# Twelve staging slots for the weights, checks made on the staged copy, and an earlier norm for the second batch

## The chip, the cores and the metric

The kernel runs on one core of a Trainium2 chip. A core has five engines that run their own instruction streams and meet at semaphores: PE (matmul), DVE (vector), ACT (activation), POOL (GpSimd), and SP, whose queue issues the DMAs here. The metric is the device time of one execution in microseconds (us); of several executions the median is given. The program is one launch, from the inputs in device memory to the output in device memory.

## What is computed

The input `x` has 16 batches of 512 rows by 512 columns. Each row is normalized; the result feeds a causal attention with 16 heads of 32 and, side by side with it, a gated feed-forward layer with 1408 inner columns. Both results are added to `x`:

```python
xn = _layernorm(x, axis=-1)
x = x + attn(xn, w_qkv, b_qkv, w_out, b_out) + ffn(xn, gate_w, up_w, down_w, gate_s, up_s, down_s)
# attn: qkv = xn @ w_qkv.T + b_qkv; softmax(q k / sqrt(32) + causal) v; out @ w_out.T + b_out
# ffn:  (silu((xn @ gate_w.T) * gate_s) * ((xn @ up_w.T) * up_s)) @ down_w.T * down_s
```

`gate_w`, `up_w` and `down_w` hold only -1, 0 and 1. The kernel computes with pairs of 16-bit floats (a high part and the rest); the three ternary matrices need only one 16-bit part, and the kernel checks while it runs that they fit into it. If a check fails, a slow general path is run instead (`general_path`).

## The kernel before, in words

`fast_path` writes one program for each engine. The work of the attention is cut into 640 **slots**, `n = 0 .. 639`: a batch is 40 slots, 4 groups `G` of 4 heads with 10 slots (`U`) each. In slot `n` PE makes one 512-wide set of scores (`scores`, L247), DVE takes the row maximum (`maximum`, L515), ACT the exponential (L436), DVE the reciprocals (L504, L506), ACT the high part of the probabilities (`high`, L428) two slots later and DVE the low part (`low`, L525). SP turns the probabilities with DMA transposes (`turn_p`, L826), and PE multiplies them by `v` (`av`). All other work hangs on slots by tables that are written out by hand: `f_at` (the gate and up products with `tanh`, `hidden`, `split_hidden`), `qk_at`, `v_at`, `av_at`, `o_at`, `d_at` (the down product), `norm_at` (the norm of the next batch), `res_at` (the load of the residual). Every engine goes through the slots in the same order and through the tables in a fixed order inside a slot, and waits in that order; so what one instruction waits for holds up all that stands behind it on its engine, the DMA issues of SP included.

**The weights** come as 49 chunks of 128 by 512 fp32 (256 KB each), in the order of `chunks`: eight chunks of `w_qkv`, then gate, up and down chunks by turns, with four more of `w_qkv` among them, and four of `w_out` last. Before the change they go through eight staging slots (`NST = 8`: the four quarters of `xnT[1]`, then `res[0..3]`). SP loads chunk `n` when chunk `n - 8` is finished (`load_weight`, L798 to L801). A "split" chunk gets its high part from ACT (L387) and its low part from DVE (L483) or POOL (L691, L693). A "plain" chunk (gate, up, down) is copied to 16 bits by ACT (gate and down, L387) or POOL (up, L687). Chunks 0 to 16 are worked on ahead of slot 0, the others two to a slot from slot 0 on (`w_slot`, `W_FIRST = 17`).

**The check** of a plain chunk (`check_plain`, L557 to L565) stands far later: in batches 1 to 11 there are three per batch, at slots 22, 28 and 34 of the batch (`check_at`). Each loads the chunk a second time into an `xin` buffer (issued by SP four slots earlier, L882), compares it on DVE with the 16-bit copy (L564), and takes the largest magnitude of the copy (`tensor_reduce`, L565).

**The norm** of batch `b` for tile `t` (128 rows): load of `x` into `xin` four slots ahead (L882), statistics on DVE (L487 to L491), the root on POOL (L735), two slots later the scaling (`scaled`, L497), then the high part on POOL (L789), the low part on DVE (L660), and at slot + 5 a DMA transpose into `xnT[b % 2]` (`turn_x`, L812). For `b >= 2` the four tiles stand at slots 0, 4, 8 and 12 of the batch before; for `b = 1` at slots 12, 14, 16 and 18 of batch 0. The first product that needs batch 1 is `qk` at slot 23.

**The stack**: the scores of a group of four heads read `stk[G % 2]`, which SP fills by 12 small DMAs from `qkp` (`stack`, L814 to L819), four in each of slots 2, 3 and 4 of the group before; one semaphore counts all twelve. The stack of group 0 is issued ahead of slot 0, between the loads of chunks 12 and 13.

## Time and profile before

| what | value |
| --- | --- |
| median of 3 runs | 2051.01 us (2050.69 to 2054.36) |
| the profiled execution, its own time | 2044.33 us |
| its span, first to last instruction | 2041.0 us |
| mean granted clock of PE, share of full | 0.98 |
| PE, DVE, ACT, POOL busy, share of the span | 93%, 83%, 65%, 49% |
| the chain that ended last: PE, DVE, SP's queue, DMA, ACT | 39%, 28%, 14%, 8%, 6% |
| slot 0 begins (first `maximum`) | 49.19 us |

The span is some 3 us shorter than the time of the same execution; what lies around it is the launch and the end. "Busy" counts the time in which an engine has an instruction in work, and DMA issues do not count. A window in the profile is a stretch of the span; below, a slot begins where its first `maximum` (L515 on DVE) begins, and windows "of slots" are cut there. The granted clock is given as a share of 2.4 GHz.

### The profile page before, as it was taken

How to read it: one execution, taken by the hardware profiler on the slowest of the kernel's cores; microseconds unless marked ns; L12 is line 12 of the kernel's file. 1: busy time of each engine (PE TensorE's matmuls, PEld its weight loads, DVE VectorE, ACT ScalarE, POOL GpSimd, SP SyncE). 2: the span in 40 equal slices, each digit the busy share in tenths (PEclk: the TensorE clock that was granted, in tenths of full speed). 3: DMA queues.
4: the chain of work that ended last, by engine and by line, in shares of the span. 5: the costliest groups of instructions: out<-in, count | busy, mean ns of one | idle time of the engine just before them, and what ended most of it. 6: DMA issues, size and time to landing. Idle time of an engine off the chain costs nothing.

```text
span 2041.0 us, 43778 instructions
## 1 busy us (share of the span) xinstructions
PE 1891.5 (93%) x14978; PEld 1225.1 (60%) x14978; DVE 1695.2 (83%) x5066; ACT 1330.5 (65%) x3723; POOL 1007.2 (49%) x1389
## 2 busy tenths in 40 slices
PE   5679999999999999999999999999999999989986
PEld 3447566665666656566665666656566665756663
DVE  3668888888888888888888898888888788888885
ACT  3747676665766667666666766666666666767673
POOL 5554554554554454554544545454554555454342
PEclk8889999999999999999999999999999999999998
DMA  6866867778677776868869787777877768676674
GB/s 196 222 125 128 185 133 163 153 136 177 134 165 146 149 162 136 179 133 163 153 135 181 139 163 150 145 175 129 180 136 161 142 137 175 130 171 122 132 147 94
DMA packets 832981, 310.24 MB, mean 152 GB/s; under 512 B 756464, under 2 KB 789232, under 8 KB 832752
## 3 DMA queue, kind: packets, MB, share of 16 engines
q1 hardware_dynamic: 832752, 307.39, 73.4%
q8 instruction: 119, 1.95, 0.4%
q14 instruction: 110, 0.90, 0.1%
HBM read 55.59 MB, written 16.78 MB: 35 GB/s over the span
## 4 chain that ended last, share of the span: by engine, by line
PE 39%; DVE 28%; SPq 14%; DMA 8%; ACT 6%; issue 4%; POOL 0%; DVEq 0%; ACTq 0%; POOLq 0%
PE bank L245 39%; SPq L819 10%; DVE phl L525 8%; DMA pt<-phl 7%; DVE bank L515 5%; ACT phl L428 4%; DVE fh L537 3%; DVE ft L533 2%; DVE small L506 2%; ACT bank L436 2%; DVE res L549 1%; SPq L826 1%; DVE small L487 1%; DVE xhl L660 1%; SPq L812 1%
## 5 line engine op out<-in xcount | busy, mean ns | idle before, releaser
L428 ACT ACTIVATE phl<-bank,small 128x512 f16<-128x512 f32 (+3 forms) x1024 | 500.2, 531 | 322.4 <-DVE small L506 217.7
L436 ACT ACTIVATE bank<-bank,small 128x512 f32<-128x512 f32 (+3 forms) x1024 | 514.4, 503 | 225.5 <-DVE small L515 218.6
L525 DVE SCALAR_TENSOR_TENSOR phl<-bank,small,phl 128x512 f16<-128x512 f32 (+3 forms) x1024 | 525.3, 544 | 102.1 <-ACT phl L428 98.3
L515 DVE CUSTOM_DVE_ANT_0 bank<-bank,mask 128x512 f32<-128x512 f32 (+3 forms) x1024 | 486.0, 505 | 109.3 <-PE bank L245 109.1
L718 POOL TENSOR_SCALAR ht<-fh 128x256 f16<-128x256 f32 x352 | 142.2, 404 | 602.1 <-DVE fh L537 602.1
L245 PE MATMUL bank<-xnT,wg 128*128 128x256 f16 x2816 | 368.0, 274 | 15.8 <-POOL wu L687 6.0
L245 PE MATMUL bank<-xnT,wu 128*128 128x256 f16 x2816 | 368.4, 274 | 0.0
L245 PE MATMUL bank<-xnT,wqkv 128*128 128x512 f16 x1536 | 355.9, 382 | 11.1 <-DMA xnT<-xhl 8.1
L245 PE MATMUL bank<-wd,ht 128*128 128x512 f16 x1408 | 330.4, 392 | 0.0
L245 PEld LDWEIGHTS bank<-xnT,wg 128*128 128x128 f16 x2816 | 262.2, 98 | 82.6 <-issue 13.2
L245 PEld LDWEIGHTS bank<-xnT,wu 128*128 128x128 f16 x2816 | 277.1, 98 | 33.5
L245 PE MATMUL bank<-stk 96*128 96x512 f16 (+3 forms) x1024 | 247.4, 303 | 51.8 <-DVE phl L525 50.9
L720 POOL TENSOR_TENSOR ht<-fh,ht 128x256 f16<-128x256 f32 x352 | 246.4, 700 | 29.4
L245 PEld LDWEIGHTS bank<-xnT,wqkv 128*128 128x128 f16 x1536 | 148.4, 98 | 179.9 <-issue 12.9
L245 PEld LDWEIGHTS bank<-wd,ht 128*128 128x128 f16 x1408 | 141.3, 101 | 167.9 <-issue 21.3
L436 ACT ACTIVATION_READ_ACCUMULATOR bank<-bank,small 128x1 f32 x1024 | 209.9, 205 | 0.0
L394 ACT ACTIVATE ft<-bank,small 128x256 f32<-128x256 f32 x352 | 168.5, 483 | 57.4 <-PE bank L245 56.9
L537 DVE SCALAR_TENSOR_TENSOR fh<-bank,small,ft 128x256 f32<-128x256 f32 x352 | 170.3, 484 | 39.2 <-DVE ft L533 1.4
L245 PE MATMUL bank<-wqkv,xnT 128*128 128x256 f16 x1536 | 179.8, 274 | 15.6 <-DMA xnT<-xhl 15.6
L245 PE MATMUL bank<-wout,att 128*128 128x512 f16 x768 | 176.1, 379 | 10.5 <-DVE res L549 7.6
L245 PEld LDWEIGHTS bank<-wqkv,xnT 128*128 128x128 f16 x1536 | 150.2, 98 | 40.2 <-DVE wqkv L483 15.5
L245 PEld LDWEIGHTS bank<-stk 96*128 96x128 f16 x1024 | 96.5, 99 | 126.2 <-DVE phl L525 68.9
(95 smaller groups left out, 1911.8 us busy)
## 6 DMA issues: line engine op xcount, KB each, us to landing
stk<-qkp SPq DMA_DIRECT2D x768, 64.0 KB, 2.1
res<-in_x_dram SPq DMA_DIRECT2D x64, 256.0 KB, 3.1
out_dram<-res SPq DMA_DIRECT2D x64, 256.0 KB, 2.4
xin<-in_x_dram SPq DMA_DIRECT2D x60, 256.0 KB, 3.2
pt<-phl SPq DMA_TRANSPOSE x512, 3.7
xin<-in_gate_dram SPq DMA_DIRECT2D x11, 256.0 KB, 3.3
xin<-in_up_dram SPq DMA_DIRECT2D x11, 256.0 KB, 3.3
xin<-in_down_dram SPq DMA_DIRECT2D x11, 256.0 KB, 3.4
```

The source lines that it names most:

```text
L245: mm = lambda o, lhs, rhs, start, stop, **k: eng.matmul(o, lhs, rhs, start=start, stop=stop, skip_group_check=True, **k)
L394: eng.activation(ft[f % 3][:, :], bank[4 + f % 2][:, 0:256], ACT.Tanh, scale=gsh[:, k:k + 1]).then_inc(a_ft, 1)
L428: i = eng.activation(phl[qt][:, j % 2, 0], pb[:, off:off + W], ACT.Copy, scale=st_r[:, c:c + 1])
L436: i = eng.activation(pb[:, off:off + W], pb[:, off:off + W], ACT.Exp, bias=st_m[:, c:c + 1], scale=-1.0, accum_out=st_s[:, c:c + 1])
L506: eng.tensor_scalar(st_r[:, c0:c0 + 4], st_r[:, c0:c0 + 4], PS, None, op0=ALU.mult).then_inc(v_rec, 1)
L515: i = eng.tensor_tensor_reduce(out=bk[:, off:off + W], in0=bk[:, off:off + W], in1=mask[:, 512 - W:512], scale=-(32.0 ** -0.5) / (QS * QS) ...
L525: i = eng.scalar_tensor_tensor(phl[qt][:, j % 2, 1], pb[:, off:off + W], st_r[:, c:c + 1], phl[qt][:, j % 2, 0], ALU.mult, ALU.subtract)
L533: eng.scalar_tensor_tensor(tt[:, :], tt[:, :], 1.0, bk[:, 0:256], ALU.add, ALU.mult).then_inc(v_fa, 1)
L537: eng.scalar_tensor_tensor(hh[:, :], bk[:, 256:512], cis[:, k:k + 1], tt[:, :], ALU.mult, ALU.mult).then_inc(v_fh, 1)
L718: eng.tensor_scalar(hs[:, 0], hh[:, :], 1.0, 1.0, op0=ALU.mult, op1=ALU.mult).then_inc(p_hh, 1)
L720: eng.tensor_tensor(hs[:, 1], hh[:, :], hs[:, 0], ALU.subtract).then_inc(p_fl, 1)
L819: eng.dma_start(stk[G % 2][32 * blk:32 * blk + 32, j], qkp[G % 2][32 * j:32 * j + 32, a:a + step + 1:step, :]).then_inc(d_stk[G % 2], 16)
```

## The change

- **Staging**: twelve slots: `res[0..3]`, four quarters of `att`, four quarters of `xnT[1]`. Chunks 0 to 23 use all twelve, chunks 24 to 48 the first eight (`slot_of`, `turn_of`, `before`, `slot_last`).
- **Copies**: POOL makes all 33 plain copies, as a clamp to -1 .. 1 (`tensor_scalar` with min and max). ACT makes only high parts of split chunks.
- **Checks**: DVE compares the staged fp32 chunk with its clamped copy right after POOL made it, in place. 12 checks (chunks 8 to 19) stand ahead of slot 0, the other 21 in slots 2 to 13, up to two to a slot. The second load and the `tensor_reduce` go, and so do `large` and two small instructions at the end. A staging slot is free for the next load only when the check is done.
- **Order ahead of slot 0**: 18 loads (before: 13) are issued ahead of the stack of group 0, and chunks up to 19 are worked on. POOL makes chunks 4 to 10 ahead of `split_qk(0, 0)`, 11 to 13 ahead of `split_qk(1, 0)`. On DVE `v_low(0, 0, 0)` stands behind the checks of chunks 8 to 10.
- **Norm of batch 1**: slots 0, 4, 8, 12, as for the other batches.
- **Stack**: in halves. A half `p` has six DMAs and a semaphore of its own, and the first five slots of a group need only half 0. The twelve DMAs stand at slots 2 (four), 3 (two), 4 (four) and 5 (two).

```diff
-            norm_at[12 + 2 * t if b == 1 else 40 * b - 40 + 4 * t] = (b, t)
+            norm_at[40 * b - 40 + 4 * t] = (b, t)
...
-    stage = [xnT[1][:, 2 * i:2 * i + 2, :].rearrange("p a b -> p (a b)").bitcast(F32) for i in range(4)]
-    stage += [res[i][:, :] for i in range(4)]
+    stage = [res[i][:, :] for i in range(4)]
+    stage += [att[:, i // 2, 2 * (i % 2):2 * (i % 2) + 2, :].rearrange("p a b -> p (a b)").bitcast(F32) for i in range(4)]
+    stage += [xnT[1][:, 2 * i:2 * i + 2, :].rearrange("p a b -> p (a b)").bitcast(F32) for i in range(4)]
...
-    W_FIRST = 17
+    W_FIRST, W_EARLY = 20, 18
+    NCH = len(chunks)
+    slot_of = [n % 12 if n < 24 else n % 8 for n in range(NCH)]
...
+    finished = [(v_plain, plains[n]) if c[0] == "plain" else ready[c[1]] for n, c in enumerate(chunks)]
...
# scores
-            w.wait_ge(d_stk[G % 2], 192 * (G // 2 + 1))
+            w.wait_ge(d_stk[2 * (G % 2) + u // 5], 96 * (G // 2 + 1))
...
# vector_program
+        def check_plain(n):
+            kind, (name, k), src, w16, lo, last = chunks[n]
+            if kind == "plain":
+                i = ("wg", "wu", "wd").index(name) * NI + k
+                w.wait_ge(p_w, gp_count[n])
+                eng.scalar_tensor_tensor(stage[slot_of[n]], stage[slot_of[n]], 1.0, w16, ALU.mult, ALU.not_equal,
+                                         accum_out=miss[:, i:i + 1]).then_inc(v_plain, 1)
...
+        for n in range(8, 11):
+            check_plain(n)
         v_low(0, 0, 0)
         for f in range(F_FIRST):
+            for n in range(11 + 3 * f, 14 + 3 * f):
+                check_plain(n)
             hidden(f)
...
-            if n in check_at:
-                check_plain(check_at[n])
+            for i in range(W_FIRST, NCH):
+                if w_slot(i) + 1 == n:
+                    check_plain(i)
...
# gpsimd_program
             if kind == "plain":
-                w.wait_ge(d_w[n % NST], 16 * (n // NST + 1))
-                eng.tensor_scalar(hi, sl, 1.0, 1.0, op0=ALU.mult, op1=ALU.mult).then_inc(p_w, 1)
-                return
+                w.wait_ge(d_w[slot_of[n]], 16 * (turn_of[n] + 1))
+                eng.tensor_scalar(hi, sl, 1.0, -1.0, op0=ALU.min, op1=ALU.max).then_inc(p_w, 1)
...
-        weight(4)
-        weight(5)
+        for n in range(4, 11):
+            weight(n)
         split_qk(0, 0)
         split_qk(0, 1)
-        for n in range(6, 11):
+        for n in range(11, 14):
             weight(n)
...
# sync_program
-        def stack(G, blk):
-            a, step = ((1, 1), (1, 2), (0, 2))[blk]
-            w.wait_ge(s_s, U * (G - 1))
+        def stack(G, p, blks):
+            w.wait_ge(s_s, U * (G - 2) + 5 * p + 5)
             w.wait_ge(p_ql, 2 * G + 2)
-            for j in range(4):
-                eng.dma_start(stk[G % 2][32 * blk:32 * blk + 32, j],
-                              qkp[G % 2][32 * j:32 * j + 32, a:a + step + 1:step, :]).then_inc(d_stk[G % 2], 16)
+            for blk in blks:
+                a, step = ((1, 1), (1, 2), (0, 2))[blk]
+                for j in (2 * p, 2 * p + 1):
+                    eng.dma_start(stk[G % 2][32 * blk:32 * blk + 32, j],
+                                  qkp[G % 2][32 * j:32 * j + 32, a:a + step + 1:step, :]).then_inc(d_stk[2 * (G % 2) + p], 16)
...
-        for n in range(8, 13):
+        for n in range(8, W_EARLY):
             load_weight(n)
-        for blk in range(3):
-            stack(0, blk)
-        for n in range(13, W_FIRST + 6):
+        stack(0, 0, (0, 1, 2))
+        stack(0, 1, (0, 1, 2))
+        for n in range(W_EARLY, W_FIRST + 4):
             load_weight(n)
+        load_x(1, 0)
...
-                if k in (2, 3, 4) and G + 1 < NGRP:
-                    stack(G + 1, k - 2)
+                if k in (2, 4) and G + 1 < NGRP:
+                    stack(G + 1, k // 4, (0, 1))
+                if k in (3, 5) and G + 1 < NGRP:
+                    stack(G + 1, k // 5, (2,))
...
-                if w_slot(i) - 3 == n:
+                if w_slot(i) - 2 == n:
                     load_weight(i)
```

The lines that begin with `#` inside the diff only name the function in which the part stands.

## Rows read from the trace of the kernel before

**Rows 1.** The page: busy time of each engine; clock in 40 slices.

```profile
PE 1891.5 (93%) x14978; PEld 1225.1 (60%) x14978; DVE 1695.2 (83%) x5066; ACT 1330.5 (65%) x3723; POOL 1007.2 (49%) x1389
...
PEclk8889999999999999999999999999999999999998
```

**Rows 2.** Windows by stage: slots 0 to 13, 14 to 23, 24 to 39.

```profile
core 0: us, PE busy (x) PEld busy (x) DVE busy (x) ACT busy (x) POOL busy (x), PEclk, DMA share, GB/s
49.20:89.40 40.20, 28.53 (x176) 17.01 (x173) 29.21 (x93) 34.30 (x92) 22.59 (x34) 0.92 0.87 219
89.40:145.30 55.90, 37.16 (x240) 21.21 (x244) 33.91 (x90) 22.30 (x62) 31.52 (x39) 0.79 0.70 149
145.30:191.60 46.30, 46.30 (x403) 31.80 (x396) 37.67 (x118) 34.72 (x98) 23.54 (x35) 1.00 0.63 125
```

**Rows 3.** Windows of slots 22 to 39: batches 1 and 13.

```profile
260.73:313.05 52.32, 51.71 (x435) 34.51 (x434) 46.90 (x142) 37.56 (x108) 26.80 (x38) 1.00 0.70 140
...
1727.97:1779.09 51.12, 51.12 (x435) 34.73 (x434) 42.45 (x134) 37.78 (x108) 25.88 (x38) 1.00 0.67 135
```

**Rows 4.** Groups: DVE checks and norms, POOL copies (count | busy us, mean ns).

```profile
L720 POOL TENSOR_TENSOR ht<-fh,ht 128x256 f16<-128x256 f32 x352 | 246.4, 700 | 29.4
...
L660 DVE TENSOR_TENSOR xhl<-xs,xhl 128x512 f16<-128x512 f32 x60 | 46.3, 772 | 8.2 <-POOL xhl L789 8.2
...
L487 DVE BATCH_NORM_STATS2 small<-xin 128x6 f32<-128x512 f32 x60 | 41.0, 684 | 0.0
...
L497 DVE TENSOR_SCALAR xs<-xin,small 128x512 f32<-128x512 f32 x60 | 38.0, 633 | 0.1
...
L564 DVE SCALAR_TENSOR_TENSOR xin<-xin,wu 128x512 f32<-128x512 f32 x11 | 12.0, 1089 | 0.0
...
L693 POOL TENSOR_TENSOR wqkv<-res,wqkv 128x512 f16<-128x512 f32 x7 | 8.4, 1197 | 0.6
...
L687 POOL TENSOR_SCALAR wu<-xnT 128x512 f16<-128x512 f32 x6 | 3.7, 616 | 0.0
```

**Rows 5.** Timeline of PE, 90 to 155 us: start us, us, instruction.

```profile
94.14 3.12 PE L245 MATMUL bank<-pt,vv 128*32 128x512 f16 x48 [8.10 <-DMA pt<-phl]
...
114.61 0.61 PE L245 MATMUL bank<-stk 96*128 96x256 f16 x2 [5.91 <-DVE phl L525]
...
139.98 5.04 PE L245 MATMUL bank<-xnT,wqkv 128*128 128x512 f16 x12 [8.09 <-DMA xnT<-xhl]
...
150.85 2.75 PE L245 MATMUL bank<-xnT,wqkv 128*128 128x512 f16 x12
```

**Rows 6.** Timeline of the SP queue: a load of x, a transpose of x.

```profile
108.20 0.33 SPq L882 DMA_DIRECT2D xin<-in_x_dram  x1
...
136.56 1.31 SPq L812 DMA_TRANSPOSE xnT<-xhl  x1
```

**Rows 7.** Windows of slots 14 to 23: batches 1 and 13.

```profile
234.60:267.56 32.96, 30.02 (x236) 18.96 (x235) 26.03 (x77) 20.05 (x57) 18.86 (x24) 1.00 0.73 161
1703.23:1732.88 29.65, 28.37 (x193) 17.80 (x194) 24.78 (x75) 19.79 (x57) 18.85 (x24) 1.00 0.81 162
```

**Rows 8.** Timeline of DVE and POOL: checks beside work of POOL.

```profile
262.72 1.39 DVE L564 SCALAR_TENSOR_TENSOR xin<-xin,wg 128x512 f32<-128x512 f32 x1
...
279.26 1.21 POOL L720 TENSOR_TENSOR ht<-fh,ht 128x256 f16<-128x256 f32 x1
279.26 0.68 DVE L564 SCALAR_TENSOR_TENSOR xin<-xin,wg 128x512 f32<-128x512 f32 x1
```

**Rows 9.** Timeline of all engines before slot 0.

```profile
13.33 0.89 POOL L691 TENSOR_SCALAR res<-res 128x512 f32<-128x512 f32 x1 [1.33 <-ACT wqkv L387]
...
20.36 0.69 DVE L543 SCALAR_TENSOR_TENSOR vv<-bank,vv 128x512 f16<-128x512 f32 x1 [4.05 <-ACT vv L415]
...
27.77 7.73 SPq L819 DMA_DIRECT2D stk<-qkp  x12
...
49.19 0.69 DVE L515 CUSTOM_DVE_ANT_0 bank<-bank,mask 128x512 f32<-128x512 f32 x1
```

More of the change, by code:

```diff
@@ L30 @@
 NHT = 14
-NST = 8
 NSTAT = 8
@@ L124, in fast_path @@
     d_small = [sem(f"d_small{i}") for i in range(5)]
-    d_w = [sem(f"d_w{i}") for i in range(NST)]
+    d_w = [sem(f"d_w{i}") for i in range(12)]
     d_x0 = [sem(f"d_x0{i}") for i in range(4)]
@@ L128, in fast_path @@
     d_xT = [sem(f"d_xT{i}") for i in range(4)]
-    d_stk = [sem(f"d_stk{i}") for i in range(2)]
+    d_stk = [sem(f"d_stk{i}") for i in range(4)]
     d_pt = [sem(f"d_pt{i}") for i in range(4)]
@@ L163, in fast_path @@
         for t in range(4):
[L164 to L173 removed]
+            norm_at[40 * b - 40 + 4 * t] = (b, t)
+    xin_load_at = {n - 4: v for n, v in norm_at.items()}
     res_at = {}
@@ L383, in weight @@
             kind, key, src, hi, lo, last = chunks[n]
-            if kind == "plain" and last != "act":
+            if kind == "plain":
                 return
-            w.wait_ge(d_w[n % NST], 16 * (n // NST + 1))
-            eng.activation(hi, stage[n % NST], ACT.Copy, scale=WS if kind == "split" else 1.0).then_inc(a_w, 1)
+            w.wait_ge(d_w[slot_of[n]], 16 * (turn_of[n] + 1))
+            eng.activation(hi, stage[slot_of[n]], ACT.Copy, scale=WS).then_inc(a_w, 1)
         def tanh(f):
@@ L470, in scalar_program @@
                 exponent(n)
-            for i in range(W_FIRST, len(chunks)):
+            for i in range(W_FIRST, NCH):
                 if w_slot(i) == n:
@@ L698, in split_qk @@
             i = 2 * G + c + 1
-            w.wait_ge(d_stk[G % 2], 192 * (G // 2))
+            for p in range(2):
+                w.wait_ge(d_stk[2 * (G % 2) + p], 96 * (G // 2))
             w.wait_ge(a_q32, i)
@@ L707, in split_av @@
             w.wait_ge(s_o, 4 * b)
+            if G == 0:
+                for i in range(4, 8):
+                    w.wait_ge(*finished[slot_last[i]])
             w.wait_ge(a_a32, G + 1)
@@ L765, in gpsimd_program @@
         for f in range(F_FIRST):
-            for n in range(11 + 2 * f, 13 + 2 * f):
+            for n in range(14 + 2 * f, 16 + 2 * f):
                 weight(n)
@@ L786, in gpsimd_program @@
                 i = 4 * b + t
-                w.wait_ge(d_xT[(i - 2) % 4], 16 * ((i - 2) // 4 + 1))
+                if t >= 2:
+                    w.wait_ge(d_xT[t - 2], 16 * (b + 1))
+                elif b >= 2:
+                    w.wait_ge(d_xT[t + 2], 16 * b)
+                else:
+                    w.wait_ge(d_xT[t], 16)
                 w.wait_ge(v_xs, i + 1)
                 eng.tensor_scalar(xhl[t % 2][:, 0], xs32[:, :], 1.0, 1.0, op0=ALU.mult, op1=ALU.mult).then_inc(p_xh, 1)
-            for i in range(W_FIRST, len(chunks)):
+            for i in range(W_FIRST, NCH):
                 if w_slot(i) == n:
@@ L798, in load_weight @@
         def load_weight(n):
-            if n >= NST:
-                w.wait_ge(*finished[n - NST])
-            eng.dma_start(stage[n % NST], chunks[n][2]).then_inc(d_w[n % NST], 16)
+            if before[n] is not None:
+                w.wait_ge(*finished[before[n]])
+            eng.dma_start(stage[slot_of[n]], chunks[n][2]).then_inc(d_w[slot_of[n]], 16)
         def turn_x(b, t, hl):
@@ L805, in turn_x @@
             if b == 1:
-                for s in range(4):
-                    w.wait_ge(*finished[stage_last[s]])
+                for i in range(8, 12):
+                    w.wait_ge(*finished[slot_last[i]])
             if b >= 2:
@@ L865, in sync_program @@
                     turn_p(G, 1, 3, n - 3)
[L866 to L867 removed]
+            for i in range(W_FIRST + 4, NCH):
+                if w_slot(i) - 2 == n:
                     load_weight(i)
             if n in xin_load_at:
[L870 to L882 removed]
+                load_x(*xin_load_at[n])
             if n - 5 in norm_at:
```

127 lines of the change are left out of this document (46 added, 81 removed).

## The prediction, made before the changed kernel ran

> **What bounds the kernel now.** I read the page first, then windows by stage, then the engines' timelines for the stretches that stand out. Over the whole span PE is busy 93% and DVE 83%, and the clock of PE is low only in the first three slices of forty and in the last [rows 1]. So most of the time is a steady state held by PE, and the start is another case. The windows say how different it is. From slot 24 of batch 0 on, PE is busy 46.30 of 46.30 us; ahead of that, slots 0 to 13 take 40.20 us with ACT busiest (34.30), and slots 14 to 23 take 55.90 us in which no engine is busy for more than 37.16, at a clock of 0.79 [rows 2]. The same ten slots of a later batch take 32.96 or 29.65 us [rows 7]. Hence some 23 us of waits in slots 14 to 23 of batch 0, and the timeline of PE names three: 8.10 us for the turned probabilities, 5.91 us for DVE's low part, 8.09 us for the turned `x` of batch 1 [rows 5]. In the second case SP's queue stood at the load of an `x` tile until 108.20, with transposes of probabilities behind it; in the third the last transpose of `x` was issued at 136.56 [rows 6], 4.7 us after PE had run dry (139.98 - 8.09 = 131.89 [rows 5]).
>
> In the steady state the windows of slots 22 to 39 tell what the late checks cost: 52.32 us in batch 1, which has them, with PE not quite full (51.71), against 51.12 us in batch 13, which has none, with PE busy for all of it [rows 3]. These two rows repeat: of the eleven batches with checks nine have 52.3 to 52.4 in these slots and two 53.4 and 53.8, of the three without two have 51.1 and one 51.5.
>
> **The parts, and what each costs.**
>
> *Late checks and their loads go* (33 comparisons, 33 `tensor_reduce`, 33 loads of 256 KB that stand in SP's queue among the transposes). They are 46.90 - 42.45 = 4.5 us of DVE per batch [rows 3], but PE hides most of it: the batch gains 52.32 - 51.12 = 1.2 us. Eleven batches: **-13.2 us**. Ends: 0 if something else fills the gap, and -16 if what the two slow windows have on top (1.1 and 1.5) goes as well. What is late next there is PE itself.
>
> *The norm of batch 1 goes to slots 0 to 12.* Its last transpose then stands at slot 17, six slots ahead of its reader, and the loads of `x` at slots 0, 4 and 8, each behind a scaling that is two slots old. Both waits of rows 6 go. The 8.10 us wait for the probabilities came from a stretch in which weights, stack and transposes were crowded into 40 us (DMA share 0.87 [rows 2]); with the same bytes over some 58 us it should go too. I take slots 14 to 23 at 32.5 us, at the slow end of rows 7 since PE comes in from a half-idle stretch: 55.9 - 32.5 = **-23.4 us**. Ends: -26.3 (29.65, the quickest later batch) and -8 (the three stalls shrink by a third only).
>
> *Slots 0 to 13 get more DVE work.* DVE was busy 29.21 us there [rows 2]. Added are 21 checks in slots 2 to 13 and most of three norm tiles: a tile is 0.68 of statistics with some 0.3 of small steps behind them (an estimate), 0.63 of scaling, 0.77 of low part [rows 4], so 3 x 2.4 = 7.2 us. What a check costs depends on POOL. One that began together with a subtraction on POOL took 0.68 us, and the subtraction 1.21 [rows 8], where the mean of its kind is 0.70 [rows 4]; one that began while POOL was adding took 1.39 [rows 8]: they do not run side by side. Alone a check costs 0.61 us from start to start of the next, at worst 1.33. POOL will be busy some 60% of this stretch (22.6 us, and 15 more copies of 0.62 and norm parts, in 58), so I take 0.9: 18.9 us. DVE's sum is 29.2 + 18.9 + 7.2 = 55.3 us, above ACT's, which loses its copies, and above PE's 28.5 [rows 2]: DVE becomes what holds these slots. At a busy share of 0.95 (0.90 is what the steady state shows beside PE [rows 3], and here nothing else is near) the stretch takes 58.5 us: **+18.3 us**. Ends: +9 (checks at 0.61, DVE never idle) and +31 (checks at 1.33, share 0.90).
>
> *The start.* POOL works on chunks 4 to 7 from 13.33 us [rows 9], four times 0.6 + 1.2 us [rows 4], then three copies: until some 23 us, where it used to idle. `v_low`, which was at 20.36 [rows 9], now stands behind the check of chunk 10 and comes at 24 to 26 us. The second `qk` product needs the bank that it frees and waits 3 to 4 us; so do the second split and the stack, issued from 27.77 before [rows 9]. Against that, gate and up chunks 11 to 15 are no longer copied behind POOL's splits of `q` and `k`, the scores need six stack DMAs and not twelve, and the gate products close up. But three checks stand ahead of each `hidden`, 12 checks in all, 8 to 11 us of DVE. No row prices the net of this. I make slot 0 begin at 47.7 and not 49.19 [rows 9]: **-1.5 us**. Ends: +3, the stack's delay carried through, and -4, a third of the 13.7 us from the stack's last issue (35.5) to slot 0 [rows 9].
>
> *The stack in halves.* In the steady state twelve issues of about 0.64 us (7.73 for twelve [rows 9]) still stand between the same two transposes. Neither old nor new wait is ever the last, since the transposes ahead of them wait for later slots. **0 us.** What hides it is that five slots lie between its landing and its reader. Two of the twelve now stand behind a transpose of `x` and a store in slot 13 of a batch, where they were ahead: if these wait, the next transpose is 1.3 us later, up to 14 times: +18, and if they don't and the order helps, as much the other way at most.
>
> *Edits that cost nothing*: slots 24 to 39 of batch 0 are full of PE before and after [rows 2]; the two small instructions fewer at the end lie beside the last output products; a norm or `att` buffer used for staging is free in time, its last chunk being checked by slot 13 and its first reader at slot 15; ACT only loses work.
>
> **The sum**: -13.2 - 23.4 + 18.3 - 1.5 = -19.8 us. The profiled execution took 2044.33 us, so 2024.5 by its measure. It was 6.7 us quicker than the median of the runs shown, 2051.01; carried over, **2031 us**. From no change a measurement of this kernel can tell about 0.2%, 4.1 us.
>
> **The rivals.**
>
> 1. *The lock.* Nearly every check runs into POOL. The copy and the next POOL instruction are back to back, so at the moment when a check is released POOL has already begun the next. For it speaks the 1.39 us of rows 8 and the mean of 1.09 over eleven [rows 4]; against it that POOL idles 40% of the stretch. Checks then cost 1.33 and slots 0 to 13 take (29.2 + 27.9 + 7.2) / 0.95 = 67.7 us, 9 more: 2040 us. The page "SBUF — State Buffer" of the Trainium skill (Who interferes with whom) states this as a rule: a vector instruction with two inputs in SBUF and a GpSimd instruction that reads SBUF shut each other out for a whole instruction, and which one waits is decided by who began. By that rule nearly every check finds POOL begun; the trace agrees on the shutting out (1.21 beside 0.68), and a chance of its own is due to it, since the change puts 33 such instructions right behind POOL's copies.
> 2. *The checks were hidden anyway.* PE is 98.8% busy in their windows, and the 1.2 us could be of another make (the load of slot 24 alone is one issue of 0.6 us ahead of a transpose). Then the steady state gives 0: 2044 us.
> 3. *Slower: the clock of PE.* In slots 0 to 13 PE has 28 us of work for 58 us. Where it had gaps before, the clock of a stretch fell to 0.79 [rows 2], and after a wait of 8 us twelve products took 5.04 us that took 2.75 a little later [rows 5]. At 1.2 GHz PE's work in slots 0 to 13 is twice 26 = 52 us, no longer hidden beside DVE, so 64 us; and slots 14 to 23, with 28.4 to 30.0 us of it at full clock [rows 7], take 60. That is +23.8 + 4.1 - 1.5 - 13.2 = +13: 2064 us. It decides when slots 0 to 23 take over 115 us together (96.1 before, plus 14.7 of gains elsewhere, plus 4.1). Against it: with 70% busy and gaps of a microsecond the clock was 0.92 in slots 0 to 13 [rows 2].
> 4. *The stack's new order delays a transpose* in each batch: +18, 2049 us.
>
> **How the numbers follow.** Forecast 0.62, with its own range 2022 to 2040 from the ends above; lock 0.17; hidden checks 0.08; clock 0.08; order 0.05. The range 2020 to 2046 holds the first three, and leaves out the clock, the order and what falls below. Faster by over 4.1 us: forecast and lock but for a little, and the hidden checks, which lie near the bound, by most: 0.84. Within it: the order and rest of these, 0.07. Slower: the clock and mishaps of the start, 0.09.
>
> **What would show it right or wrong.** Slot 0 at 46 to 49 us; DVE busy over 90% in slots 0 to 13, 55 to 62 us long; slots 14 to 23 within 30 to 36 us, without the waits for the turned `x` and for probabilities; slots 22 to 39 at 51.1 to 51.5 in every batch from 1 to 14. I am wrong if the stretch 0 to 13 passes 70 us, if stalls stay in 14 to 23, or if a steady batch stays at 52.3.

## The result, and the profile after

The changed kernel takes 2016.72 us (median of 4 runs, 2012.53 to 2020.36), the kernel before in the same comparison 2052.69 us: a ratio of 0.9824, interval 0.98 to 0.9847. That is 31 to 41 us less where 20 were forecast, and the median lies below the forecast range. The profiled executions, 2012.53 and 2044.33 us, are compared below; their spans differ by 30.1 us. The executions of one kernel differ by some 10 us, and the longer ones have the lower mean clock. The profiled one of before is a quick one: its mean clock is 0.980, and of the 71 executions of before that were timed beside the experiments one has more (0.983) and 70 have 0.979 or less. So the profiled pair shows 31.8 us where the medians show 36.0. Two more executions of before, of 2213 and 2813 us at mean clocks of 0.844 and 0.654, are left out everywhere.

From the page of the kernel after: busy time by engine, the clock in 40 slices, and the chain that ended last.

```profile
PE 1877.6 (93%) x14978; PEld 1224.9 (61%) x14978; DVE 1669.5 (83%) x5031; ACT 1319.1 (66%) x3701; POOL 1018.7 (51%) x1411
...
PEclk9799999999999999999999999999999999999998
...
PE 60%; DVE 19%; SPq 7%; DMA 4%; ACT 3%; issue 2%; POOL 2%; DVEq 0%; POOLq 0%; ACTq 0%
```

Beside [rows 1] the totals hardly move: 14 us less of PE, 26 of DVE. The chain moved: PE held 39% of it before and holds 60% now; SP's queue fell from 14% to 7%. Where the time went is read from the stages. Windows after: batch 0 (slots 0 to 13, 14 to 23, 24 to 39), then slots 22 to 39 of batches 1 and 13.

```profile
core 0: us, PE busy (x) PEld busy (x) DVE busy (x) ACT busy (x) POOL busy (x), PEclk, DMA share, GB/s
50.24:109.58 59.34, 36.67 (x222) 20.65 (x223) 55.62 (x151) 28.88 (x79) 44.25 (x56) 0.75 0.84 190
109.58:139.97 30.39, 26.30 (x170) 15.58 (x172) 24.42 (x75) 20.23 (x59) 23.71 (x30) 1.00 0.75 148
139.97:186.30 46.33, 46.33 (x403) 31.80 (x398) 37.66 (x119) 34.58 (x98) 23.93 (x36) 1.00 0.68 135
256.86:307.98 51.12, 51.12 (x435) 34.73 (x434) 42.42 (x134) 37.73 (x108) 25.87 (x38) 1.00 0.68 134
1698.32:1749.84 51.52, 51.19 (x435) 34.84 (x434) 42.31 (x134) 37.83 (x108) 25.88 (x38) 1.00 0.67 131
```

The first three answer to [rows 2], the last two to [rows 3]. Slots 0 to 13 are 19.1 us longer, with DVE busy 94% of them; slots 14 to 23 are 25.5 us shorter and the clock there is 1.00 where it was 0.79. Batch 1 now takes in slots 22 to 39 the 51.12 us that batch 13 took before.

All stages of all kernels are in the next table. Its stage times are in us, are differences of slot starts in the trace (a slot starts with its first row maximum) and come from one execution of each kernel; the ratio comes from all. "Stretches" counts, in batches 1 to 14, the stretches in which PE's granted clock is 1.2 GHz instead of 2.4.

| kernel | slot 0 at | batch 0: 0–13 | 14–23 | batches 1–14: 0–13 | 14–21 | 22–39 | stretches | ratio (95%) |
| --- | --- | --- | --- | --- | --- | --- | --- | --- |
| before | 49.2 | 40.2 | 55.8 | 603.6 | 375.9 | 730.9 | 8 | 1 |
| after | 50.2 | 59.3 | 30.4 | 601.9 | 365.7 | 717.2 | 4 | 0.9824 (0.98–0.9847) |
| e8 after again | 50.3 | 59.3 | 30.4 | 602.5 | 366.3 | 716.7 | 4 | 0.9844 (0.9799–0.989) |
| e1 no late checks | 51.0 | 39.0 | 56.9 | 602.8 | 376.0 | 717.9 | 8 | 0.9908 (0.9888–0.9928) |
| e2 halves | 51.5 | 39.1 | 56.9 | 603.6 | 382.3 | 732.1 | 12 | 1.0005 (0.9988–1.0022) |
| e3 after, whole stack | 52.5 | 59.4 | 30.4 | 602.8 | 375.8 | 716.6 | 7 | 0.9862 (0.9842–0.9881) |
| e12 = e1 + e2 | 49.3 | 39.1 | 55.4 | 602.5 | 366.6 | 717.1 | 5 | 0.988 (0.9847–0.9913) |
| e13 e2, loads moved | 48.9 | 39.5 | 56.5 | 603.3 | 368.1 | 743.9 | 5 | 1.0022 (1.0006–1.0039) |
| e4 norm late | 51.6 | 53.6 | 50.3 | 602.8 | 363.7 | 716.9 | 3 | 0.9889 (0.9862–0.9916) |
| e6 unchecked | 41.5 | 44.3 | 33.9 | 602.7 | 365.3 | 717.9 | 5 | 0.9733 (0.9688–0.9779) |
| e7 v_low first | 48.3 | 59.4 | 33.3 | 602.8 | 363.9 | 717.8 | 4 | 0.9831 (0.9792–0.9869) |
| e5 half 1 late | 51.7 | 59.4 | 30.4 | 601.9 | 388.5 | 728.1 | 14 | 0.9974 (0.9951–0.9998) |
| e9 half 1 in 7, 8 | 50.0 | 59.4 | 32.1 | 602.8 | 365.7 | 717.9 | 10 | 0.9762 (0.9746–0.9779) |
| e10 late only | 42.1 | 43.4 | 35.2 | 603.8 | 372.1 | 724.8 | 9 | 0.978 (0.9759–0.98) |
| e11 = e10 + e9 | 39.6 | 45.5 | 35.8 | 604.1 | 357.7 | 725.9 | 7 | 0.9688 (0.9669–0.9708) |
| e14 e11, loads moved | 42.4 | 45.3 | 34.1 | 604.0 | 355.5 | 728.9 | 7 | 0.9721 (0.9692–0.9751) |
| e15 e11 again | 41.5 | 44.0 | 34.7 | 604.0 | 356.1 | 728.9 | 7 | 0.9707 (0.9677–0.9737) |

Slots 24 to 39 of batch 0 are 46.3 to 46.4 us in all but e5 (47.0), and what lies behind batch 14 is 134.7 to 142.8 us. For the change itself the stages give +1.0 (slot 0), +19.1, -25.4, -1.7, -10.2, -13.7 and +0.8 (behind batch 14): -30.1 us, the whole difference of the spans. The -10.2 us in slots 14 to 21 of the steady batches have no term in the forecast.

### The profile page after: what moved, and what is told of

It reads as the page before. It is cut to its first block, busy times and chain, and to the rows that moved or that the text cites. A ratio compares the mean times of both kernels' runs of the same rounds, so it can differ in the third digit from the quotient of the medians.

```text
span 2010.9 us, 43751 instructions
## 1 busy us (share of the span) xinstructions
PE 1877.6 (93%) x14978; PEld 1224.9 (61%) x14978; DVE 1669.5 (83%) x5031; ACT 1319.1 (66%) x3701; POOL 1018.7 (51%) x1411
## 4 chain that ended last, share of the span: by engine, by line
PE 60%; DVE 19%; SPq 7%; DMA 4%; ACT 3%; issue 2%; POOL 2%; DVEq 0%; POOLq 0%; ACTq 0%
PE bank L245 60%; DVE phl L528 5%; SPq L815 5%; DMA pt<-phl 4%; DVE bank L518 4%; ACT phl L428 2%; DVE fh L540 2%; DVE ft L536 1%; DVE res L552 1%; DVE small L509 1%; ACT bank L436 1%; DVE xhl L651 1%; DVE small L490 1%; DVE xs L500 1%; SPq L889 1%
## 5 line engine op out<-in xcount | busy, mean ns | idle before, releaser
L709 POOL TENSOR_SCALAR ht<-fh 128x256 f16<-128x256 f32 x352 | 142.8, 406 | 558.3 <-DVE fh L540 558.3
L245 PE MATMUL bank<-wd,ht 128*128 128x512 f16 x1408 | 322.8, 386 | 0.0
L245 PE MATMUL bank<-stk 96*128 96x512 f16 (+3 forms) x1024 | 245.9, 301 | 56.7 <-DVE phl L528 56.5
L711 POOL TENSOR_TENSOR ht<-fh,ht 128x256 f16<-128x256 f32 x352 | 241.6, 686 | 29.4
L721 POOL TENSOR_TENSOR res<-res,dtmp 128x512 f32<-128x512 f32 x64 | 81.1, 1268 | 192.7 <-DVE dtmp L558 192.6
```

The lines of the kernel that those rows point to most:

```text
L245: mm = lambda o, lhs, rhs, start, stop, **k: eng.matmul(o, lhs, rhs, start=start, stop=stop, skip_group_check=True, **k)
L709: eng.tensor_scalar(hs[:, 0], hh[:, :], 1.0, 1.0, op0=ALU.mult, op1=ALU.mult).then_inc(p_hh, 1)
L711: eng.tensor_tensor(hs[:, 1], hh[:, :], hs[:, 0], ALU.subtract).then_inc(p_fl, 1)
L721: eng.tensor_tensor(res[t][:, :], res[t][:, :], dtmp[:, :], ALU.add).then_inc(p_dy, 1)
```

## The experiments

### Which part gives what: e1, e2, e3 and e12

e1 is the kernel before without the late checks (the gate, up and down weights go unchecked). e2 is the kernel before with the stack in halves, e3 the kernel after with the whole stack of before.

```diff
# e1, on the kernel before
-            check_at[40 * (b + 2) - 18 + 6 * r] = i
# e2, on the kernel before (e3 is the reverse, on the kernel after)
-                if k in (2, 3, 4) and G + 1 < NGRP:
-                    stack(G + 1, k - 2)
+                if k in (2, 4) and G + 1 < NGRP:
+                    stack(G + 1, k // 4, (0, 1))
+                if k in (3, 5) and G + 1 < NGRP:
+                    stack(G + 1, k // 5, (2,))
```

> The kernel before, with the 33 late checks and their loads left out (so the plain weights are not checked at all); nothing else changes. The changed kernel's batches 1 to 14 took 1684.8 us against 1710.4 before, -25.6. Theory A (the late checks are all of it): this kernel gains 24 to 27 us, ratio 0.987 to 0.988, with slots 14 to 21 of batches 1 to 14 at 366 us in sum (before 376) and slots 22 to 39 at 717 (before 731). Theory B (the checks give the 13.2 us of the prediction, and the stack in halves gives the rest): ratio 0.993 to 0.994, slots 14 to 21 stay at 376. Theory C (slots 14 to 21 are a matter of which stretches of the clock fall to a half, and that is chance from kernel to kernel): slots 22 to 39 at 717, and slots 14 to 21 anywhere from 364 to 376, following the number of half-clock stretches in slot 19 (8 before, 4 after) at 1.7 us each.

> The kernel before, with only the stack in halves (order, waits and semaphores as in the changed kernel). Prediction's term: 0 us in the steady state, start within 1 us. Theory A: ratio 0.999 to 1.001. Theory B: 10 to 12 us quicker, ratio 0.994 to 0.995, with slot 17 of batches 1 to 14 shorter than its 5.3 us on average. Theory C: slots 14 to 21 move with the number of half-clock stretches only.

> The changed kernel with the stack whole again (four DMAs in each of slots 2, 3 and 4, one semaphore per buffer). Theory A: as the changed kernel, ratio 0.982 to 0.984, slots 14 to 21 at 366 us in sum. Theory B: 10 to 12 us lost, ratio 0.987 to 0.989, slots 14 to 21 back to 376. The start: slot 0 within 1 us of 50.2 if the whole stack was not what the first scores waited for.

e1 moves slots 22 to 39 from 730.9 to 717.9 us, e2 gives nothing, and e3 loses 10.1 us in slots 14 to 21 (365.7 to 375.8) and a ratio of 0.9862 for 0.9824. The runs bear out e3's loss: its five executions (2021.35 to 2026.31 us) all lie above the eight of the changed kernel in its two comparisons (2012.16 to 2020.36). Its slot 0 came 2.3 us later than in the changed kernel, where within 1 us was expected. e1 gains 19 us by its ratio and only 10.8 by its span, since the profiled execution of before is a quick one. What the late checks cost is in two slots: 22 and 23 together take 6.83 us in each batch of before that has checks and 4.90 in the others.

So in the profiled executions the halves are worth nothing in one kernel and 10 us in the other. Either they need the late checks gone, or the norm's slots or the staging. e12 has e1's and e2's edits together and nothing else.

> The kernel before with two edits together: the 33 late checks with their loads and reductions left out (the gate, up and down weights go unchecked), and the stack in halves. Alone, the first gave 0.9908, the second 1.0005. Theory (the halves pay only where the late checks are gone): slots 14 to 21 of batches 1 to 14 fall from 376 us in sum to 364 to 368, slots 22 to 39 stay at 717 to 719, the half-clock stretches in those batches are 3 to 5 and not 8, and the ratio is 0.984 to 0.987. Rival (the two edits add up, and the 10 us in slots 14 to 21 come from the new norm slots or the staging): slots 14 to 21 at 376 to 382, ratio 0.990 to 0.992.

Slots 14 to 21 fall to 366.6 us with 5 stretches, so norm and staging aren't needed for that. That the two edits interact is seen in these single executions and not settled by the runs: e12 lies 5.7 us below e1 by the ratios (0.988 for 0.9908) with intervals that overlap, and the profiled execution of e12 has the highest clock of its six (0.982, the others 0.974 to 0.981), that of e2 the lowest of its twelve (0.973, up to 0.977). The ratio, 0.988, is above the band that was expected; its interval holds it.

A smaller part of the gain needs no such partner. Slot 17, in sum over the 14 batches, is 74.4 us in before and 72.5 in e2, 72.7 in e1 and 70.9 in e12, 74.2 in e3 and 71.4 in after: in each pair the halves take 1.8 to 2.8 us off it. The rest is the clock. Windows of e12: slots 14 to 21 of batch 3, then of batch 5, and slots 17 to 19 of batch 5.

```profile
477.34:504.50 27.16, 24.60 (x152) 14.82 (x150) 19.44 (x60) 16.57 (x46) 16.56 (x21) 0.94 0.86 160
720.41:745.54 25.13, 23.03 (x153) 14.48 (x151) 19.63 (x59) 16.51 (x46) 16.56 (x21) 1.00 0.87 170
729.08:738.92 9.84, 7.74 (x49) 4.44 (x47) 7.04 (x25) 5.90 (x18) 5.80 (x7) 1.00 1.14 185
```

The same of e2: slots 14 to 21 of batch 3, then slots 17 to 19.

```profile
482.34:509.42 27.08, 24.75 (x153) 14.92 (x151) 19.49 (x60) 16.63 (x46) 16.60 (x21) 0.94 0.83 170
491.04:502.48 11.44, 9.11 (x46) 4.55 (x45) 6.87 (x24) 6.74 (x20) 5.86 (x7) 0.85 1.03 196
```

The amount of work is the same; the windows differ in the clock. With a stretch at 1.2 GHz slots 17 to 19 have a mean of 0.85 and PE is busy 9.11 us for what takes 7.74 at full clock. Such a stretch makes slot 19 some 1.7 us longer (4.24 to 4.58 for 2.92 us in the batches of the kernels before and after). The 7 stretches between e2 and e12 are most of their 15.7 us in slots 14 to 21: slot 19 alone is 61.4 us in sum in e2 and 48.9 in e12.

### What stands in slot 17: e5 and e9

In before, after, e1, e2, e3, e12 and e13 each stretch begins within 1.5 us of the end of a wait of PE, and that wait stands in slot 17 in all but one case. Timelines after, batch 2: SP's queue, ACT, PE.

```profile
353.35 2.56 SPq L815 DMA_DIRECT2D stk<-qkp  x4
355.95 0.59 SPq L889 DMA_DIRECT2D res<-in_x_dram  x1
356.58 1.54 SPq L815 DMA_DIRECT2D stk<-qkp  x2
358.24 5.66 SPq L822 DMA_TRANSPOSE pt<-phl  x3
```

```profile
362.90 0.69 ACT L428 ACTIVATE phl<-bank,small 128x512 f16<-128x512 f32 x1 [4.76 <-DMA pt<-phl]
```

```profile
364.43 0.39 PE L245 MATMUL bank<-stk 96*128 96x256 f16 x2 [2.82 <-DVE phl L528]
```

Read upwards: PE waits for DVE's low part, DVE for ACT's high part, ACT 4.76 us for the transpose that frees its `phl` buffer, and that transpose stood in SP's queue until 358.24 behind the stack's issues. The same wait of PE, 1.3 to 4.1 us long, stands in slot 17 of every batch from 1 to 14, in before, after, e2, e12 and e13. e5 and e9 move the second half's six issues away from it.

```diff
-                if k in (2, 4) and G + 1 < NGRP:
-                    stack(G + 1, k // 4, (0, 1))
-                if k in (3, 5) and G + 1 < NGRP:
-                    stack(G + 1, k // 5, (2,))
+                if k in (2, 3) and G + 1 < NGRP:
+                    stack(G + 1, 0, ((0, 1), (2,))[k - 2])
# e5
+                if k == 0 and G:
+                    stack(G, 1, (0, 1, 2))
# e9
+                if k in (7, 8) and G + 1 < NGRP:
+                    stack(G + 1, 1, ((0, 1), (2,))[k - 7])
```

> The changed kernel with the second half of a stack issued in slot 0 of its own group (six DMAs), five slots ahead of its reader; slots 2 and 3 of the group before keep only the first half. So six issues and not twelve (3.7 us less) stand ahead of the transpose that ACT waits for in slot 17 of every batch (14 waits, 63.5 us in sum in the changed kernel, PE idle for 58.8 us in batches 1 to 14). Theory Q (SP's queue ahead of that transpose makes the stall, and the stall makes PE's clock fall in slot 19): slot 17 of batches 1 to 14 falls from 71.4 us in sum to 35 to 45, the half-clock stretches (4 there) all but go, and the kernel is 25 to 45 us quicker than the changed one, ratio to the kernel before 0.961 to 0.970. Rival P (the halves only shift when the clock's stretches fall, the queue does not matter): within 5 us of the changed kernel, slot 17 stays at 70. Rival R (the six issues in slot 0 delay the three transposes behind them, and the wait turns up in slots 10 to 14): the same sum elsewhere, ratio 0.98 or above.

> The changed kernel with the second half of a stack issued in slots 7 (four) and 8 (two) of the group before, behind the transposes of slot 7 and ahead of that of slot 9, where SP's queue has nothing else; slots 2 and 3 keep the first half. With that half in slot 0 the wait went from slot 17 (71.4 to 32.8 us in sum over batches 1 to 14) to slot 14 (2.34 to 6.26 us each). Theory Q (it is the number of issues just ahead of a transpose whose landing someone waits for): slot 17 at 33 to 45 us in sum and slot 14 still at 2.3 to 2.6 each, slots 14 to 21 at 325 to 345 in sum (366 before), no or few half-clock stretches in batches 1 to 14; 20 to 40 us quicker than the changed kernel, ratio 0.963 to 0.973. Rival R2 (the landing in slots 8 and 9 of the issues delays the transpose of slot 9, and with it the probabilities of two slots later in the next group): slots 10 to 13 or 20 to 23 longer by 2 us each, ratio 0.98 or above.

Both take the wait of slot 17 away (the slot falls from 71.4 us over 14 batches to 32.8 and 32.9), and both put one into slot 14. PE in slot 14 of batch 2, after:

```profile
348.35 1.81 PE L245 MATMUL bank<-pt,vv 128*32 128x512 f16 x48 [1.05 <-issue]
```

In e5:

```profile
354.61 3.39 PE L245 MATMUL bank<-pt,vv 128*32 128x512 f16 x48 [4.55 <-DMA pt<-phl]
```

In e9:

```profile
348.43 3.35 PE L245 MATMUL bank<-pt,vv 128*32 128x512 f16 x48 [2.44 <-issue]
```

In e5 the six issues stand right ahead of the transposes that slot 14 reads: 4.55 us of waiting, a stretch in every batch, slots 14 to 21 at 388.5 us; the late issue gives all back and more, as rival R had it. In e9 the wait is shorter, but in 10 of 14 batches the products behind it still run wholly or mostly at half clock (3.06 to 3.39 us for 1.81), and slots 14 to 21 stay at 365.7 us. Both miss the 20 to 45 us that theory Q expected: it was right that the queue makes the wait of slot 17, and didn't see that the issues would be paid for in slot 14. What e9 gains over after in the ratio (0.9762 for 0.9824) hardly shows in its profiled execution, which is only 1.8 us shorter in span: that one is the slowest of its five, with a mean clock of 0.977 where the others have 0.980 to 0.982.

### Does the load at slot 18 keep the halves from paying: e13

```diff
# on e2
-            check_at[40 * (b + 2) - 18 + 6 * r] = i
+            check_at[40 * (b + 2) - 14 + 4 * r] = i
```

> The kernel before with the stack in halves, and with the three late checks of a batch at slots 26, 30 and 34 instead of 22, 28 and 34, so that their loads are issued at slots 22, 26 and 30: none of them stands in SP's queue in slots 14 to 21 any more. With the halves alone the ratio was 1.0005, slots 14 to 21 of batches 1 to 14 took 382 us in sum with 12 half-clock stretches. Theory L (the load issued at slot 18 is what keeps the halves from paying): slots 14 to 21 fall to 364 to 370 us, the stretches to 3 to 6, slots 22 to 39 stay at 730 to 733, ratio 0.992 to 0.996. Rival D (it is DVE's work for the checks, or their traffic, wherever they stand in the batch): slots 14 to 21 stay at 376 to 382, the stretches at 8 to 12, ratio 0.999 to 1.002.

The stage goes by theory L, to 368.1 us with 5 stretches, and the runs agree: the mean clock is 0.977 to 0.982 in e13's twelve executions and 0.973 to 0.977 in e2's twelve. The total goes by the rival, with a ratio of 1.0022. Slots 22 to 39 of batch 1, e13:

```profile
259.95:313.56 53.61, 51.87 (x435) 34.41 (x434) 46.58 (x143) 37.61 (x108) 26.73 (x38) 1.00 0.73 138
```

At slots 26, 30 and 34 the three checks cost 53.61 - 51.12 = 2.5 us a batch and not 1.2 [rows 3], 11.8 us over the eleven batches, which takes back nearly all of the 14.2 gained. SP's queue in slots 18 and 19 shows the issue in question; e2, batch 2; its window from the clock's fall to that issue (mean clock 0.50); then e13.

```profile
373.97 1.34 SPq L813 DMA_TRANSPOSE xnT<-xhl  x1
375.36 0.58 SPq L886 DMA_DIRECT2D xin<-in_gate_dram  x1
375.98 3.03 SPq L828 DMA_TRANSPOSE pt<-phl  x1
```

```profile
372.78:375.36 2.58, 2.58 (x9) 0.93 (x7) 2.55 (x9) 2.50 (x8) 0.00 (x0) 0.50 0.84 187
```

```profile
371.67 1.35 SPq L813 DMA_TRANSPOSE xnT<-xhl  x1
373.06 2.31 SPq L828 DMA_TRANSPOSE pt<-phl  x1
```

From kernel to kernel the stretches go with the load at slot 18: with halves and no load at slot 18 (after, e4, e6, e7, e8, e12, e13) there are 3 to 5 stretches; with the load, with the whole stack, or with both (before, e1, e2, e3, e10) 7 to 12. How the load could do it is open, and the nearest reading, that its issue brings the stretch, is wrong: the clock falls first. In e2's batch 2 it is down from 372.78 us and the load is issued at 375.36; in each of the ten batches of e2 that have both, the fall is 2.0 to 3.6 us ahead of the load. In batches 12 to 14, which have no load, before and e2 have two stretches each and e10 has one. PE's wait ahead of the fall is as long in e2 (2.92 us, batch 2) as in batches of after without a stretch (2.82 us). e13 also moved two of the comparisons, so that slots 22 and 23 take 4.90 us and not 6.83. That a stretch depends on the moment at which a batch's wait comes, which any edit inside a batch shifts, is a rival that no run here tests.

### The norm, the early checks, the start: e4, e6, e7

```diff
# e4, on the kernel after
-            norm_at[40 * b - 40 + 4 * t] = (b, t)
+            norm_at[12 + 2 * t if b == 1 else 40 * b - 40 + 4 * t] = (b, t)
# e6, on the kernel after
-    finished = [(v_plain, plains[n]) if c[0] == "plain" else ready[c[1]] for n, c in enumerate(chunks)]
+    finished = [ready[c[1]] for c in chunks]
...
-            check_plain(n)
# e7, on the kernel after
+        v_low(0, 0, 0)
         for n in range(8, 11):
             check_plain(n)
-        v_low(0, 0, 0)
```

> The changed kernel with the norm of batch 1 back at slots 12, 14, 16 and 18. The prediction gave the move of the norm the largest part of the 23.4 us in slots 14 to 23 of batch 0. If that is right: slots 0 to 13 get some 7 us shorter (59.3 to about 52), and slots 14 to 23 go from 30.4 to 45 to 50, with the 8 us wait for the turned x back at slot 23: 9 to 12 us slower than the changed kernel in all, ratio 0.987 to 0.988. Rival: the stalls were made by the crowd of weight loads alone, and DVE's slower pace in slots 0 to 13 cures them whatever the norm does: then the two changes cancel, within 3 us of the changed kernel.

> The changed kernel with all 33 comparisons left out (the plain weights are not checked; a staging slot is free once POOL has copied). The prediction priced 21 checks at 0.9 us of DVE each in slots 0 to 13 and called DVE the bound there. If so: slots 0 to 13 go from 59.3 us to 38 to 43, slot 0 begins at 46 to 48 and not at 50.2, and in all 16 to 24 us go, ratio 0.971 to 0.975. Rival: POOL, which now makes all copies, or the loads hold these slots too: slots 0 to 13 stay above 50 and fewer than 10 us go.

> The changed kernel with v_low(0, 0, 0) ahead of the checks of chunks 8 to 10. In the changed kernel PE waits 1.76 us for it at 26.26, the second split and the stack start at 31.76 and not at 27.77, and slot 0 at 50.2. If that wait leads to slot 0: slot 0 begins at 47 to 49, 1.5 to 3 us quicker in all. Rival: the checks of chunks 14 to 19 between the hidden steps lead to slot 0, so it moves by less than 0.7 us.

e4 has slots 14 to 23 of batch 0 at 50.3 us for 30.4, and slots 0 to 13 at 53.6 for 59.3: moving the norm is worth 14.2 us net in these slots and 12.7 in the span, where 9 to 12 were expected. e6 leaves all checks of the ternary weights out. Its span is 19.7 us shorter: slot 0 comes 8.7 us earlier and slots 0 to 13 take 44.3 us, with DVE no longer full. Slot 0 came 4.5 us earlier than expected and slots 0 to 13 took 1.3 more than the band, so the early checks cost more ahead of slot 0 than was thought. Windows of e6: slots 0 to 13 and 14 to 23 of batch 0.

```profile
41.51:85.81 44.30, 27.59 (x170) 16.08 (x167) 35.23 (x109) 27.36 (x76) 35.96 (x55) 0.90 1.07 263
85.81:119.66 33.85, 31.54 (x240) 20.03 (x244) 25.33 (x75) 22.25 (x61) 25.20 (x32) 0.93 0.90 177
```

e7 brings slot 0 forward by 2.0 us and finds 2.9 more in slots 14 to 23: no gain.

What a check costs beside POOL is in the timeline after, 31.7 to 35.5 us.

```profile
31.70 0.61 POOL L675 TENSOR_SCALAR wg<-xnT 128x512 f16<-128x512 f32 x1
32.28 0.61 POOL L675 TENSOR_SCALAR wu<-res 128x512 f16<-128x512 f32 x1
32.35 1.08 DVE L485 SCALAR_TENSOR_TENSOR xnT<-xnT,wg 128x512 f32<-128x512 f32 x1 [6.24 <-POOL wg L675]
32.85 1.05 POOL L675 TENSOR_SCALAR wd<-res 128x512 f16<-128x512 f32 x1
33.37 1.08 DVE L485 SCALAR_TENSOR_TENSOR res<-res,wu 128x512 f32<-128x512 f32 x1
```

A check released at 32.35 finds POOL's next copy begun at 32.28 and takes 1.08 us instead of 0.68; the copy behind it, at 32.85, takes 1.05 instead of 0.61. The two engines alternate. The Trainium skill, "SBUF — State Buffer", section Who interferes with whom, states the exclusion (for a vector instruction with two inputs in SBUF and a GpSimd instruction that reads SBUF) and that issue order decides who blocks; both rows agree. Both sides pay here in turn, which the forecast counted on one side only.

### Checks late again, but on the new staging: e10, e11, e14, e15

e10 takes all checks out of the start and puts one comparison each (no `tensor_reduce`, since the clamp bounds the copy) at slots 23, 32 and 34 of batches 1 to 11, with loads at slots 18, 28 and 29. e11 adds e9's stack. Both check all weights.

```diff
# on the kernel after; the early check_plain calls go
+        check_at[40 * (b + 1) + (23, 32, 34)[r]] = i
+        check_load[40 * (b + 1) + (23, 32, 34)[r]] = 40 * (b + 1) + (18, 28, 29)[r]
...
+            w.wait_ge(d_xin[use % 2], 16 * (use // 2 + 1))
+            eng.scalar_tensor_tensor(xi[:, :], xi[:, :], 1.0, w16, ALU.mult, ALU.not_equal, accum_out=miss[:, i:i + 1]).then_inc(v_plain, 1)
# e14, on e11
-        check_at[40 * (b + 1) + (23, 32, 34)[r]] = i
+        check_at[40 * (b + 1) + (26, 30, 34)[r]] = i
-        check_load[40 * (b + 1) + (23, 32, 34)[r]] = 40 * (b + 1) + (18, 28, 29)[r]
+        check_load[40 * (b + 1) + (26, 30, 34)[r]] = 40 * (b + 1) + (22, 26, 30)[r]
```

> The changed kernel with no check on the staged copy; instead the 33 comparisons stand in batches 1 to 11 again, three to a batch, as comparisons alone (POOL's clamp makes the tensor_reduce needless), at slots 23, 32 and 34, with their loads at slots 18, 28 and 29, none ahead of the transposes of slots 5 to 7 of a group. Without any check the kernel was 19.7 us quicker by its trace than with the early ones. In the kernel before a batch paid 1.2 us for its late checks, in slots 22 to 39. If what it paid for was the load in slot 24 and the two reduces, slots 22 to 39 stay at 717 to 722 us in sum and the kernel is 14 to 20 us quicker than the changed one, ratio 0.973 to 0.977. If any DVE work in these slots costs: 728 to 731, ratio 0.979 to 0.981.

> Both: late comparisons as in e10_late_only and the second half of the stack in slots 7 and 8. If the two add up: ratio 0.955 to 0.963, some 80 us quicker than the kernel before. If PE, once it is full in every slot, makes DVE the next to wait for: no more than half of the smaller gain on top of the larger.

> e11 (late comparisons on the clamped copies, second half of the stack in slots 7 and 8) with the three loads at slots 22, 26 and 30 and the comparisons at 26, 30 and 34. Theory L: slots 14 to 21 fall from 357.7 us, where one load stood at slot 18, to 350 to 355, ratio 0.965 to 0.968. Rival D: they stay at 356 to 360, ratio 0.968 to 0.971. One execution of e11 took 6940.59 us; the fast path cannot, so it points to the general path: if the comparisons at their new places raise the flag again, an execution near 6940 us comes back here or in e15.

> e11 word for word. If its one execution of 6940.59 us came from an order in the program that fails now and then, it comes back in some of these executions; if all lie at 1985 to 1997 us, it stays a single event of unknown cause. The ratio repeats at 0.967 to 0.971.

e10 gets nearly all of e6's start (slot 0 at 42.1, slots 0 to 13 in 43.4 us) and pays 7.6 us in slots 22 to 39 (724.8 for 717.2) and 6.4 in slots 14 to 21, where there are 9 stretches, 8 of them in slots 17 and 18. The 724.8 us lie between what was expected if the load of slot 24 and the reduces were the price (717 to 722) and if any DVE work were (728 to 731). e11, without the wait of slot 17, has 357.7 us in slots 14 to 21; the median of its five executions at the usual length is 1989.67 us and the ratio 0.9688, short of the 0.955 to 0.963 that was expected if the two gains add up; e15, the same kernel, gave 0.9707 (0.9677 to 0.9737). It is faster than both kernels, by 3% against before and by 1.2 to 1.6% against after.

One execution of e11, out of six, took 6940.59 us at a mean granted clock of 1.0. No other execution of any kernel here is longer than 2814 us, so most likely the general path ran because a check raised its flag; that isn't shown. None of the four executions of e15 and the four of e14 did so (1988.79 to 1995.54 us). The cause stays open, and until it is found e11 is a measurement and not a kernel to use. e9, which checks as the changed kernel does, beats both with no such event in five executions. e14, with that load moved, has 355.5 us in slots 14 to 21, and e15, with the load at slot 18, has 356.1: where the wait of slot 17 is gone, the place of the load makes no difference that these runs show, in the stage or in the ratio (0.9721 and 0.9707). Theory L expected 350 to 355.

e8 is the changed kernel once more:

> The changed kernel once more, beside the others, so that the parts can be compared on one chip. The clock theory expects slots 14 to 21 of batches 1 to 14 at 364 to 370 us with 3 to 6 half-clock stretches, and ratio 0.980 to 0.985; if it shows 8 or more stretches, the difference between the kernels with 4 and those with 8 was chance.

It has 366.3 us in slots 14 to 21, 4 stretches and a ratio of 0.9844, all inside what was expected.

## Why the prediction was right or wrong

**The late checks** (-13.2): right. Slots 22 to 39 gave -13.7, e1 alone -13.0. The price is made in slots 22 and 23 (6.83 us for 4.90), and part of it is made up behind them. The rival by which they were hidden anyway is out.

**The norm of batch 1** (-23.4): right, -25.4 with the rest of the staging. The waits for the turned `x` and for the turned probabilities are gone, what PE still waits there is 4.0 us for DVE's low part, and the clock came back to 1.00. e4 shows that the norm's own part is -19.9 in these slots and +5.7 in slots 0 to 13.

**Slots 0 to 13** (+18.3, DVE 55.3 us, share 0.95): +19.1, DVE 55.62 us, share 0.94. The price of a check, 0.9, was 0.92 from start to start of the next (21 checks). Rival 1 was right that most checks are locked out, 14 of the 21 took 1.08 us or more and 6 took 0.68 or 0.69; what it had wrong is the price, since a check of 1.08 us costs 1.02 from start to start and not 1.33. POOL was busy 75% of the stretch and not 60%. (55.3 / 0.95 is 58.2 us and not 58.5, so the term should have read +18.0.)

**The start** (-1.5): +1.0. The wait of `qk` was 1.76 us and not 3 to 4, but the stack was issued from 31.76 and not from 27.77 [rows 9], and e6 prices the early checks at 8.7 us of start. The forecast had their sum, 8 to 11 us, and wrote it off against other gains. Slot 0 at 50.24 lies outside its 46 to 49.

**The clock in batch 0** (rival 3, 2064 us): it fell in slots 0 to 13, to 0.75, lower than before, as the rival said; PE's work there rose from 28.53 us [rows 2] to 36.67 but stayed below DVE's 55.62. It did not last into slots 14 to 23, where PE was busy 87% at full clock. The deciding point, 115 us for slots 0 to 23, was never near (89.7).

**The step that failed** is "The stack in halves", in its words "Neither old nor new wait is ever the last, since the transposes ahead of them wait for later slots. **0 us.**" In slot 17 of every batch from 1 to 14 the transposes were the last: PE waits behind them, and what stands ahead of them in SP's queue counts (e5 and e9 took over 38 us off slot 17 by moving six issues). The step put that wait at nothing, and with it what the clock does behind it. The forecast shows no row of slots 14 to 21 of a steady batch by themselves; rows 7 were read only as a price for batch 0. Of the 3.3 us by which they differ, 1.9 are the check in slots 22 and 23 and 1.4 are slots 14 to 21 (26.1 and 24.8 us), which go from 24.8 to 28.5 us among the batches of before. The clock row of the page hides the falls, for a slice of 51 us with one stretch of 3.4 us at half clock still reads 9. The forecast named the order of the queue as worth 18 us either way, gave a chance to the loss and none to the gain.

Measured is -10.2 in these slots: 3.0 in slot 17, where the halves have their part in every pair, and most of the rest in slot 19 (53.3 to 47.5 us in sum), with 4 stretches for 8. In the profiled executions the halves give +6.4 while the loads are there (382.3 for 375.9) and -9.4 when they are gone (366.6 for 376.0). By the ratios they give +1.0 us in e2, -5.7 from e1 to e12, and -3.7 to -7.8 from e3 to the changed kernel. The gain in the changed kernel is thus shown; how much of it needs the late checks gone isn't, and why the clock falls in some batches and not in others stays open.

Of the gap of 10.3 us between -19.8 and -30.1, slots 14 to 21 are 10.2. The rest is small (minus: worse than forecast): start -2.5, slots 0 to 13 -0.8, slots 14 to 23 +2.0, slots 22 to 39 +0.5, slots 0 to 13 of later batches +1.7, the end -0.8. Another 1.7 us lie outside the spans, and carrying the 6.7 us from profile to median cost 2.5, since the profiled execution of the new kernel lies only 4.2 us below its median. Together that is the distance from 2031 to 2016.72.

## What to carry to other kernels

Open each stage of the steady state in which no engine is full, also where the change seems not to touch it: a wait of 2 to 3 us per batch can turn an edit priced at nothing into 10 us. A plain DMA issue takes some 0.4 to 0.6 us of its queue here (medians by line, kernel after), and the question for a moved one is which transfer behind it is read first; moved away from slot 17 they were paid in slot 14. Check such edits in pairs, in a two-by-two of kernels, before adding up their gains, and compare the mean clocks of all executions before reading a stage of one: here a profiled execution was the quickest or the slowest of its kernel more than once.
